# A recurrent layer, two feed-forward layers and an attention on one core: gate weights folded in another stage, and smaller blocks in one level of a triangular inverse

## The reference

```python
x = x + attn_a(layernorm(x))   # delta rule: 8 heads of 128, two keys per step
x = x + ffn(layernorm(x))      # 256 -> 512 -> 512 -> 256, relu
x = x + attn_b(layernorm(x))   # 16 heads, 4 groups of keys, causal
x = x + ffn(layernorm(x))
```

```python
q_flat, v_flat = h @ Wq, h @ Wv
gate  = q_flat @ Wg            # (2048, 4)
delta = v_flat @ Wd            # (512, 4)
bias  = sigmoid(gate) * delta  # a key counts where bias > 0
```

## Time and profile before

| | us |
|---|---|
| median of 3 runs | 4434.16 (4428.42 to 4441.27) |
| the profiled execution | 4430.39 |
| its span, first to last instruction | 4428.5 |
| table stage and its end | about 0 to 143 |
| delta rule | about 143 to 2525 |
| feed-forward f | about 2525 to 2865 |
| attention | 2865 to about 3980 |
| feed-forward h | about 3980 to 4428.5 |

### The profile page before, as it was taken

How to read it: one execution, slowest core, us unless ns; L and a number is a source line. 1 busy time by engine, 2 the same in 40 slices (tenths; PEclk the granted TensorE clock), 3 DMA queues, 4 the chain that set the end, 5 groups by cost and what they waited for, 6 DMA issues and landing times. The chain is left out here.

```text
span 4428.5 us, 96953 instructions
## 1 busy us (share of the span) xinstructions
PE 4126.1 (93%) x32143; PEld 3443.9 (78%) x32143; DVE 2977.5 (67%) x7897; ACT 2185.5 (49%) x5661; POOL 1582.6 (36%) x2836
## 2 busy tenths in 40 slices
PE   4699999999999999999999689789999999999979
PEld 3488888888888888888888578767777777777768
DVE  4577777777777777777777354346776776776655
ACT  2355555555555555555555144334444444444444
POOL 0466666666666666666666100000000000000000
PEclk9999999999999999999999699979999999999989
DMA  3333333333333333333333232121111111111021
GB/s 134 92 80 89 79 80 89 87 91 88 79 90 83 79 89 79 89 84 91 92 79 83 71 120 86 58 63 47 52 32 53 52 47 37 52 47 47 10 69 34
DMA packets 545328, 321.37 MB, mean 73 GB/s; under 512 B 251584, under 2 KB 503488, under 8 KB 543296
## 3 DMA queue, kind: packets, MB, share of 16 engines
q1 hardware_dynamic: 544832, 315.12, 25.0%
HBM read 230.95 MB, written 83.98 MB: 71 GB/s over the span
## 5 line engine op out<-in xcount | busy, mean ns | idle before, releaser
L938 DVE SCALAR_TENSOR_TENSOR g_conv<-g_r,g_taps,g_conv 128x511 f32<-128x511 f32 (+2 forms) x961 | 699.0, 741 | 133.9 <-ACT g_conv L821 125.4
L825 ACT ACTIVATE g_us<-g_chn 128x128 f32<-128x128 f32 x528 | 146.6, 278 | 678.2 <-PE g_chn L620 677.4
L1990 ACT ACTIVATE a_pr<-a_pr,a_low 128x128 f32<-128x128 f32 (+3 forms) x512 | 286.5, 560 | 391.1 <-DVE a_low L2135 375.0
L2295 POOL TENSOR_TENSOR a_dg<-a_const,a_fl 128x384 fp32r<-128x384 f32 x32 | 26.5, 827 | 1156.2 <-DVE a_fl L2142 1156.2
L545 PE MATMUL g_r<-g_x_hi,g_w_hi 128*128 128x512 f32 x770 | 365.8, 475 | 9.7 <-issue 7.4
L2135 DVE CUSTOM_DVE_ANT_0 a_pr<-a_sc,a_bias 128x128 f32<-128x128 f32 (+3 forms) x512 | 242.0, 485 | 191.0 <-issue 172.2
L545 PE MATMUL g_r<-g_x_hi,g_w_lo 128*128 128x512 f32 x770 | 306.2, 398 | 0.0
L545 PE MATMUL g_r<-g_x_lo,g_w_hi 128*128 128x512 f32 x770 | 304.0, 395 | 0.0
L1809 PE MATMUL a_out<-a_pt,a_v 128*128 128x512 f32 (+3 forms) x1024 | 298.0, 434 | 0.9 <-DVE a_oT L2155 0.9
L1138 POOL TENSOR_TENSOR g_prod<-g_small 64x14 f32<-64x14 f32 (+6 forms) x896 | 227.7, 254 | 170.1 <-DMA g_small<-lower_d 104.4
L821 ACT ACTIVATE g_conv<-g_r,g_taps 128x512 f32<-128x512 f32 x321 | 220.5, 687 | 135.9 <-PE g_r L545 124.8
(11 more groups left out here) (357 smaller groups left out, 12085.3 us busy)
## 6 DMA issues: line engine op xcount, KB each, us to landing
g_w_raw<-w_heads SPq DMA_DIRECT2D x66, 768.0 KB, 4.9
lower_d<-g_L SPq DMA_DIRECT2D x64, 512.0 KB, 3.4
g_T<-low_d SPq DMA_DIRECT2D x64, 512.0 KB, 5.1
g_U<-upp_d SPq DMA_DIRECT2D x64, 512.0 KB, 6.4
a_w<-w_groups SPq DMA_DIRECT2D x32, 640.0 KB, 4.6
oT_d<-g_oT SPq DMA_DIRECT2D x67, 256.0 KB, 6.4
f_oT<-oT_d SPq DMA_DIRECT2D x8, 2048.0 KB, 8.5
a_wo<-wo_b SPq DMA_DIRECT2D x32, 512.0 KB, 5.4
```

The source lines that it names most:

```text
L938: ins = V.scalar_tensor_tensor(out=y[:, k:L], in0=x[:, 0:L - k], scalar=tap, in1=y[:, k:L], op0=ALU.mult, op1=ALU.add)
L1990: A(pr[g % 2][:, i, 0:width(i)], pr[g % 2][:, i, 0:width(i)], ACT.Exp, scale=-1.0, bias=low[g % 2][:, i:i + 1], accum_out=tot[g % 2][:, i: ...
```

## The change

Two edits that have nothing to do with each other.

1. `Wq @ Wg` and `Wv @ Wd` are made at the end of the table stage. The four inputs are loaded on SP's queue before the last two batches' turns, 40 matmuls with 4 moving columns stand on PE between the last batch and the matmuls that wait for g, ACT copies the result, SP stores it to `gd_d`, and `attention` loads its 8 KB instead.
2. The first level of the inverse works in four diagonal blocks of 32 rows: 32x32 stationary, 16 moving columns, 16 matmuls (32 records) for a half. The mask's row of constants and the two DVE operations shrink to 16 columns for a chunk, and `lev_add` takes four operations of 32 partitions for a half. The second level is as before.

```diff
+        BLOCKS = {l: [slice(i, i + (2 << l)) for i in range(0, P, 2 << l)] for l in LEVELS[:-1]}
...
-                    for r in QUADS:
-                        mm = M.matmul(lev[hf][r, c, 0:HCOL].rearrange("p (j n) -> p j n", n=1 << l), Lm[o][r, hf * HC + c, r],
-                                      seconds(U[o][r, hf * HC + c, r], l), start=True, stop=True)
+                    for r in BLOCKS[l]:
+                        mm = M.matmul(lev[hf][r, c, 0:1 << l], Lm[o][r, hf * HC + c, r], U[o][r, hf * HC + c, r.start + (1 << l):r.stop], start=True, stop=True)
...
-                    for r in QUADS:
-                        mm = M.matmul(lev[hf][r, c, 0:HCOL], T[r, hf * HC + c, r], nu[r, hf * HC + c, 0:HCOL], start=True, stop=True)
+                    for r in BLOCKS[l]:
+                        mm = M.matmul(lev[hf][r, c, 0:1 << l], T[r, hf * HC + c, r], nu[r, hf * HC + c, 0:1 << l], start=True, stop=True)
...
-                    V.tensor_tensor(half(nu, hf)[:, :, 0:HCOL], lev[hf][:, :, 0:HCOL], levels[:, li, 0:HCOL].unsqueeze(1).to_broadcast([P, HC, HCOL]),
+                    n = 1 << l
+                    V.tensor_tensor(half(nu, hf)[:, :, 0:n], lev[hf][:, :, 0:n], levels[:, li, 0:n].unsqueeze(1).to_broadcast([P, HC, n]),
...
-                    for r in QUADS:
-                        to = blk(half(U[o], hf)[r, :, r], l, 1)
-                        ins = V.tensor_tensor(to, to, packed(lev[hf][r, :, 0:HCOL], l), ALU.add)
+                    for r in BLOCKS[l]:
+                        to = half(U[o], hf)[r, :, r.start + (1 << l):r.stop]
+                        ins = V.tensor_tensor(to, to, lev[hf][r, :, 0:1 << l], ALU.add)
```

The table stage and the start of the attention:

```diff
+            for to, name in ((wq, "wqT"), (wv, "wvT"), (wg, "wg"), (wd, "wd")):
+                sp.dma_start(to[:], io[name].rearrange("(p n) d -> p n d", p=P)).then_inc(s["t_gw"], 16)
             for par in (0, 1):
                 turn(B - 2 + par, par, False)
             store_rows(B, 1)
+            sp.wait_ge(s["t_gd"], 1)
+            sp.dma_start(io["gd_d"], gd[:].rearrange("p k n -> p (k n)")).then_inc(s["t_out0"], 16)
...
+            pe.wait_ge(s["t_sig"], B + 1)
+            pe.wait_ge(s["t_gw"], 64)
+            for k in range(KD):
+                for first, w, v, many in ((0, wq, wg, NQ), (HKV, wv, wd, HKV)):
+                    at = k * 2 * HKV + first
+                    for n in range(many):
+                        mm = nc.tensor.matmul(ps_ab[:, at:at + HKV], w[:, n, k * P:(k + 1) * P], v[:, n, :], start=(n == 0), stop=(n == many - 1))
+            mm.then_inc(s["t_gm"], 1)
             pe.wait_ge(s["t_g"], 1)
...
+            act.wait_ge(s["t_gm"], 1)
+            nc.scalar.activation(gd[:].rearrange("p k n -> p (k n)"), ps_ab[:, 0:KD * 2 * HKV], ACT.Copy).then_inc(s["t_gd"], 1)
...
+            sp.dma_start(gd[:].rearrange("p k n -> p (k n)"), io["gd_d"]).then_inc(s["in"], 16)
             sp.dma_start(const[:], io["consts"]).then_inc(s["in"], 16)
...
-            for i in (0, 1):
-                sp.dma_start(pr[i][:].rearrange("p m (j d) -> p (m j) d", d=D), io["wqT"][i * NQ * P // 2:(i + 1) * NQ * P // 2]
-                             .rearrange("(n p) d -> p n d", p=P)).then_inc(s["in"], 16)
...
-            pe.wait_ge(s["in"], 16 * 6)
...
+            pe.wait_ge(s["in"], 32)
...
+            dve.wait_ge(s["in"], 32)
+            V.tensor_copy(gd_hi[:], gd[:]).then_inc(s["gd_hi"], 1)
+            dve.wait_ge(s["gd_hi"], 1)
+            V.tensor_tensor(gd_lo[:], gd[:], gd_hi[:], ALU.subtract).then_inc(s["gd_lo"], 1)
```

More of the change, by code:

```diff
@@ L70, in constants @@
         s = 1 << l
[L71 to L74, removed]
+        for at in range(0, P, 2 * s):
+            lev[at:at + s, i, 0:s] = -1.0
     put("levels", lev.reshape(P, len(LEVELS) * C))
@@ L145, in build_tables @@
         start = sb("t_start", [P, 8])
+        NQ = HKV * G
+        wq, wv = sb("t_wq", [P, NQ, D]), sb("t_wv", [P, HKV, D])
+        wg, wd = sb("t_wg", [P, NQ, HKV]), sb("t_wd", [P, HKV, HKV])
+        gd = sb("t_gd", [P, KD, 2 * HKV])
         ps_x = ps("t_ps_x", [P, 2, L])
@@ L196, in _ @@
             sp.dma_start(io["tab_d"][:, BH:BH + 1, :], flat[:, 0:1, :]).then_inc(s["t_out0"], 16)
-            sp.wait_ge(s["t_out0"], 32 * (B // 2) + 32 + 1)
+            sp.wait_ge(s["t_out0"], 32 * (B // 2) + 48 + 1)
             sp.wait_ge(s["t_out1"], 32 * (B // 2) + 32 + 1)
@@ L324 @@
 T_SEMS = ["t_const", "t_x0", "t_x1", "t_xT", "t_out0", "t_out1", "t_tab", "t_init", "t_xn", "t_tr", "t_ab", "t_g", "t_sum", "t_A",
-          "t_mv", "t_std", "t_sig", "t_beta", "t_abs", "t_exp", "t_dec", "t_dve", "t_xlo", "t_xhi", "t_glo", "t_move"]
+          "t_mv", "t_std", "t_sig", "t_beta", "t_abs", "t_exp", "t_dec", "t_dve", "t_xlo", "t_xhi", "t_glo", "t_move", "t_gw", "t_gm", "t_gd"]
 K0, K1, V0, V1, QB, GB = range(6)
@@ L418, in blk @@
             return m.rearrange("p c (n k) -> p c n k", k=2 * size)[:, :, :, second * size:(second + 1) * size]
-        HCOL = C // 2
         QUADS = (slice(0, C), slice(C, P))
-        def seconds(m, l):
-            return m.rearrange("p (n k) -> p n k", k=2 << l)[:, :, 1 << l:2 << l]
+        BLOCKS = {l: [slice(i, i + (2 << l)) for i in range(0, P, 2 << l)] for l in LEVELS[:-1]}
         def packed(m, l):
@@ L583, in lev_un @@
                         continue
-                    for r in QUADS:
-                        mm = M.matmul(lev[hf][r, c, 0:HCOL], T[r, hf * HC + c, r], nu[r, hf * HC + c, 0:HCOL], start=True, stop=True)
+                    l = LEVELS[li]
+                    for r in BLOCKS[l]:
+                        mm = M.matmul(lev[hf][r, c, 0:1 << l], T[r, hf * HC + c, r], nu[r, hf * HC + c, 0:1 << l], start=True, stop=True)
                 mm.then_inc(s["d_un"], 1)
@@ L1598, in attention @@
         LAST = B * HKV - 1
-        wg, wd = sb("wg", [P, NQ, HKV]), sb("wd", [P, NK, HKV])
+        gd = sb("gd", [P, KD, 2 * HKV])
         gd_hi, gd_lo = (sb(f"gd_{i}", [P, KD, 2 * HKV], F32R) for i in ("hi", "lo"))
@@ L2262, in _ @@
             query(0, 1)
-            dve.wait_ge(s["in"], 16 * 6)
             diagonal(0, 0, 0, 0, 16)
@@ L2304, in turn @@
                         pool.wait_ge(s["lg"], G * TT * t)
-                    else:
-                        pool.wait_ge(s["gd"], 1)
                     spread(1 - n % 2, (n + 1) % HKV, nb, 8 * b - 8 * bp + 16 if n < HKV - 1 else 8 * b + 8 * bp + 16)
             spread(0, 0, 0, 16)
-            pool.wait_ge(s["in"], 16 * 6)
+            pool.wait_ge(s["in"], 32)
             loop(pool, turn)
 ATTN_SEMS = ["xl", "x0", "x1", "in", "w", "wv", "wo0", "wo1", "out0", "out1", "kept", "kb0", "kb1",
-             "gd", "gd_hi", "gd_lo", "tr", "x_hi", "x_lo", "gt", "gc", "sig", "keep", "vp", "v", "vtp", "vtT", "dg", "one", "w_hi", "w_lo", "wv_hi", "wv_lo",
+             "gd_hi", "gd_lo", "tr", "x_hi", "x_lo", "gt", "gc", "sig", "keep", "vp", "v", "vtp", "vtT", "dg", "one", "w_hi", "w_lo", "wv_hi", "wv_lo",
              "mv", "std", "xn", "k", "kT", "k_hi", "q_hi", "q", "qT", "sc", "lg", "ex", "nrm", "ptr", "pta", "ptv", "pv", "oT", "fl", "ftr", "frow",
@@ L2388 @@
     io["tab_d"] = nc.dram_tensor("tab_d", (P, B * H + 1, 5 * NC), F32).ap()
+    io["gd_d"] = nc.dram_tensor("gd_d", (P, KD * 2 * HKV), F32).ap()
     io["oT_d"] = nc.dram_tensor("oT_d", (B * H + 3, P, L), F32).ap()
```

3 lines of the change are left out of this document (removed).

## The result

| | kernel before | changed kernel |
|---|---|---|
| median of 7 runs, us | 4435.75 (4428.42 to 4447.64) | 4412.79 (4404.31 to 4415.74) |
| ratio, 95% interval | | 0.994 (0.9928 to 0.9953) |
| span of the profiled execution, us | 4428.5 | 4411.0 |

The change makes the kernel faster, by 23 us between the medians and 27 by the ratio. The forecast was 4436 us, +1.4, "same". The time lies 0.8 us inside the range given, and the sign was wrong.

A forecast was written before the change was run, and what follows sets the result against it. PE was taken to set the pace, in the delta rule with few waits behind DVE. 15.6 + 10 - 24.2 = +1.4 us gave 4435.6 us, say 4436; own range 4418 to 4460, stated range with rivals 4412 to 4535.

The forecast's parts named there:

- 16 ns a record: First inverse level on PE: expected pace of the 32-column blocks, two overlapping, making a group 0.50 us instead of 0.44.
- the bounds from the same split: First level's pace with no fixed part, 13.4 ns (-0.03 us a group), or 8 ns fixed, 17.4 ns (+0.10).
- term of +15.6 us on PE: First level's groups on PE: 260 groups, each 0.06 us longer.
- rival 2: First level: four blocks overlap, not two; 8 ns a record, 0.25 us a group, 4387 us in all; chance 0.13.
- the pace of 29.4 is just that of one block's load for a whole matmul: Old first level: one matmul's second half seems to run beside the next's first half, which four blocks would not change.
- Rival 1: First level: small-block records still cost 29.4 ns each, a group 0.91 us, 4532 us in all; chance 0.27.
- lev_add and lev_T: First level on DVE: adds of 220 ns, four a half, end later, so PE's `lev_T(0)` waits 0.15 us more.
- term of +10 us on the end: New wait of `lev_T(0)` for DVE's adds, 0.15 us in each of 65 turns.
- The attention: Attention's start: without the weight products PE starts earlier, -24.2 us, bounds -12 to -26.
- The table stage: End of the table stage: the moved products take 17.05 us within PE's wait for g, 7 us of cover left, cost 0.
- +25.6 for the level: First level of the inverse as a whole: 15.6 us for PE's groups and 10 us for the wait on DVE.
- the lowest sum of the bounds, 4418: Low end of the forecast's own range: +8 us for the level and -24 for the attention, -16 us in all.

The follow-up runs named there:

- the operation moved: Guard operation put ahead of the next unit's first convolution, still on DVE; against the kernel before: changed kernel 0.9884 (-51 us), kernel before 1.002 (+9 us).
- on ScalarE: Guard operation made by ScalarE behind its squares instead of by DVE; against the kernel before: changed kernel 0.9898 (-45 us), kernel before 1.0013 (+6 us).
- the fold alone: Kernel before with only the weight products moved from the attention to the table stage, first level unchanged; 0.9934 of the kernel before, -29 us.
- two and two: Changed kernel, each first-level group's 32 matmuls issued in two runs of sixteen, each alternating between two blocks; 0.9962 of the kernel before, -17 us.
- block by block: Changed kernel, all eight chunks of one 32x32 block issued before the next block's; 1.0277 of the kernel before, +123 us.

## Why the prediction was wrong

**The step that failed** is "A block of 32 columns should then take 26.7 ns and about 5, and overlapped in twos as now, 16 ns a record." No run shows the parts of that price, 26.7 ns and a fixed rest of 5, on which the sum's 16 ns stands, nor the bounds from the same split (13.4 and 17.4 ns): they were my estimate. The runs show the whole: 31 to 32 ns a record for one block (the estimate's two parts add up to 31.7), 16 for two, 8 for four. So 16 ns would have been right for two blocks. What failed is "in twos as now": this loop issues four different blocks one after another, all four run side by side, and a record comes every 8 ns. The sum's term of +15.6 us on PE (+0.06 a group) is in truth -0.18 a group, -47 us on PE, of which a turn sees 0.55 us, 65 x 0.55 = 36. The argument against rival 2, "the pace of 29.4 is just that of one block's load for a whole matmul", took an equality of two numbers for a mechanism. Its counterpart stood in the trace: the records' starts before come in pairs 7 ns apart and then 52 ns later, one record of each block every 58 to 59 ns. The third level's single block of 64 has the same 58 to 59 ns with twice the moving columns, so the halving was overlap and not the narrower operand. The forecast read only the mean.

**Rival 1** (each record keeps its 29.4 ns, 4532 us) is refuted by the same row: 8.4 ns a record for 32x32x16 in four blocks.

**lev_add and lev_T.** Right in mechanism: 216 ns an operation (220 expected), `lev_T(0)` waits for DVE. From `chain_R(6)` to `lev_T(0)` it is now 1011.33 - 1010.11 = 1.22 us, expected 1.25, and 1.04 before. But taking the adds away gives an undisturbed turn 0.10 us and no measurable time, so the term of +10 us on the end is at most some 7.

**What the sum left out:** the collision of DVE's guard operation with POOL. Without it the changed kernel is 20 to 24 us faster (the operation moved) or 14 to 18 (on ScalarE). It was in the trace before, as the wait of 15.1 us for `chain_S`: the prediction names the row and does not ask why DVE is late. Rival 2's 4387 us was off for this: its mechanism holds, and with the operation out of its old place the medians are 4384 and 4395.

**The attention.** Right: -24.2 forecast, 24.1 at the first transpose; the stage is 21.1 us shorter in the profiled pair and 24.6 in the profile of the fold alone, whose time measures -29 (-35 to -23). **The table stage.** Right: cover of 7 us, cost 0 (140.4 and 140.9 us). Loads went out behind the stores and held nothing up.

So two errors cancelled in part: the level's groups came out cheaper than forecast, and the collision took most of that back. The forecast's +25.6 for the level is in truth -5 with the collision and about -20 without it. That the time lies inside the range is luck: its lower end of 4412 has no term behind it (it is said to leave out the lowest bounds, and takes them in), and the lowest sum of the bounds, 4418, is 5 us above what was measured.

## What to carry to other kernels

The small matmuls on different diagonal blocks of the array overlapped here as far as the order of issue let them (8.4 ns a record with four blocks in rotation, 13.2 two and two, 22.6 block by block): read the single starts and not the mean pace, of a forecast's rows and of an experiment's alike, and put matmuls of different blocks next to each other. When an edit shortens PE's path, look at what was waiting or colliding at its end, in operations that the edit doesn't touch: a 0.15 us operation whose median is 0.38 is already a warning. The small guard operation of VectorE, with its inputs in SBUF, was held at the end of the turn beside GpSimd for up to 2.6 us in place of 0.15, and moving it brought 20 to 24 us, as much as the faster level; in the kernel before the same move brought no time (+9 us). So look for such an operation in such a place. Where a time and the turns in its profile disagree by a few us, compare the granted clocks of the executions first.

## What the runs showed of the hardware

- 32x32x16 matmuls in fp32: one diagonal block takes a record every 31 to 32 ns (after a first step of 53), and different blocks run side by side, 7 ns apart, so four in rotation take one every 8 ns. Over a group of 32 records the mean is 8.4 ns (four, the changed kernel), 13.2 (two and two) and 22.6 (block by block), since the next block starts while the one ahead is half done. A block of 64 takes one every 58 to 59 ns in the kernel before, after a first step of 79 ns with 32 moving columns (in a pair, L564) and of 107 with 64 (alone, L561).
- A 128x4 operation of DVE from SBUF to SBUF (`qden`) lasted 0.15 us alone and up to 2.6 us in its old place (3.6 once moved, in the kernel before), ending within 0.05 us of the end of an operation of POOL whenever it lasted over 0.3 us, after one to four of them in a row; TENSOR_SCALAR (up to 2.6 us) and SCALAR_TENSOR_TENSOR with two inputs from SBUF (up to 2.3) alike. `convolve`, which reads PSUM, kept its duration: 731 to 752 ns in 882 cases of the changed kernel, 338 of them begun beside an operation of POOL.
- With the same matmuls block by block the granted clock of the delta rule (300 to 2400 us) was 0.96, with PE busy for 2073 of 2100 us in the records; in the changed kernel it was 1.00, with PE busy for 2040.
- Over the 12 executions with the operation on ScalarE in the kernel before, and the 17 of the kernel before beside them, 0.001 less of the mean granted clock went with 3 to 5 us more, of some 4440.
